# Two heads in one exponential: neighbouring PSUM banks read together in an attention stage

## The reference

```python
def _L0_attn_ref(hidden_states, cos, sin, wq, bq, wk, wv, bv, wo, bo):
    q = (hidden_states @ wq + bq).reshape(B, T, NH, HD).transpose(0, 2, 1, 3)
    k = (hidden_states @ wk).reshape(B, T, NH, HD).transpose(0, 2, 1, 3)
    v = (hidden_states @ wv + bv).reshape(B, T, NH, HD).transpose(0, 2, 1, 3)
    q, k = apply_rope(q, k, cos, sin)
    scale = 1.0 / jnp.sqrt(jnp.float32(HD))
    scores = jnp.einsum('bhqd,bhkd->bhqk', q, k) * scale
    attn = jax.nn.softmax(scores, axis=-1)
    out = jnp.einsum('bhqk,bhkd->bhqd', attn, v)
    out = out.transpose(0, 2, 1, 3).reshape(B, T, H)
    return out @ wo + bo

x = x + _L0_attn_ref(_layernorm(x), ...)
x = x + _L0_ffn_ref(_layernorm(x), ...)   # 16 experts, each takes its 128 best tokens of a batch; one shared expert
```

## Time and profile before

| | us |
|---|---|
| median of 3 runs | 2427.51 (2425.11 to 2431.14) |
| span of the profiled execution | 2427.3 |
| PE busy in the span | 2283.2 (94%) |
| DVE busy | 1891.8 (78%) |
| ACT busy | 1632.3 (67%) |
| POOL busy | 886.1 (37%) |

### The profile page before, as it was taken

One profiled execution on the slowest core, in us unless ns is written; L12 is line 12 of the kernel. 1 busy time (PEld: TensorE's weight loads), 2 busy tenths in 40 slices (PEclk: granted clock), 3 DMA queues, 4 the chain that ended last, 5 costly groups with the idle time before them and its releaser, 6 DMA issues. The chain is left out here.

```text
span 2427.3 us, 44076 instructions
## 1 busy us (share of the span) xinstructions
PE 2283.2 (94%) x16398; PEld 1340.3 (55%) x16398; DVE 1891.8 (78%) x3506; ACT 1632.3 (67%) x3168; POOL 886.1 (37%) x1223
## 2 busy tenths in 40 slices
PE   5899999999999999999999988899997999999996
PEld 4233334334334334334333323788886888888886
DVE  5999999999999999999999994466654555555553
ACT  2599999999999999999999987323323343333432
POOL 4051451451451451441542220000003666666664
PEclk8799999999999999999999999799998999999998
DMA  2000011010010010010010010332322545454443
GB/s 76 1 18 1 1 36 36 1 50 22 1 55 17 9 61 3 19 53 1 19 36 1 19 36 18 126 100 78 104 61 81 115 109 112 87 112 113 100 99 35
DMA packets 104364, 122.74 MB, mean 51 GB/s; under 512 B 7553, under 2 KB 91393, under 8 KB 104193
## 3 DMA queue, kind: packets, MB, share of 16 engines
q1 hardware_dynamic: 79616, 86.90, 11.2%
q0 software_dynamic: 24576, 33.57, 8.1%
HBM read 78.50 MB, written 41.94 MB: 50 GB/s over the span
## 5 line engine op out<-in xcount | busy, mean ns | idle before, releaser
L474 DVE TENSOR_REDUCE sb_MX<-ring 128x1 f32<-128x512 f32 x2048 | 1284.5, 681 | 82.0 <-PE ring L782 65.4
L606 ACT ACTIVATE sb_PR<-rot 128x512 f32<-128x512 f32 x2048 | 1123.3, 621 | 102.8 <-PE rot L793 92.3
L782 PE MATMUL ring<-sb_KT,sb_QT 32*128 32x512 bf16 x2048 | 517.1, 390 | 48.9 <-DVE sb_MX L474 36.5
L804 PE MATMUL pv<-sb_PR,sb_VA 128*32 128x512 f32 x4096 | 547.0, 606 | 2.9 <-ACT sb_OT L661 0.6
L782 PEld LDWEIGHTS ring<-sb_KT,sb_QT 32*128 32x128 bf16 x2048 | 128.1, 91 | 632.9 <-DVE sb_MX L474 565.8
L793 PE MATMUL rot<-sb_QT,sb_KT 32*128 32x512 bf16 x2048 | 422.1, 386 | 1.6
L1095 ACT ACTIVATE ex_GL<-ex_gu 128x512 f32<-128x512 f32 x128 | 76.4, 597 | 347.4 <-PE ex_gu L63 345.2
L1162 DVE TENSOR_TENSOR ex_HF<-ex_GL,ex_gu 128x512 f32<-128x512 f32 x128 | 87.5, 684 | 250.8 <-ACT ex_GL L1095 250.8
L1059 POOL DMA_INDIRECT out<-ex_YS,ex_rows_out x128 | 208.8, 1631 | 44.3 <-issue 43.8
L1016 POOL TENSOR_TENSOR ex_pool_scratch<-identity 128x1 f32<-128x1 f32 x96 | 35.1, 366 | 477.6 <-POOLq L859 332.0
L61 PE MATMUL ex_gu<-ex_XH,weights_high 128*128 128x512 f32 x512 | 200.4, 391 | 2.4 <-DVE ex_XL L1154 2.4
(11 more groups left out here) (168 smaller groups left out, 4272.2 us busy)
## 6 DMA issues: line engine op xcount, KB each, us to landing
sb_XA<-x SPq DMA_DIRECT2D x8, 1024.0 KB, 5.5
sb_XR<-x SPq DMA_DIRECT2D x8, 1024.0 KB, 5.8
out<-sb_XR SPq DMA_DIRECT2D x8, 1024.0 KB, 4.5
xn<-sb_XN SPq DMA_DIRECT2D x8, 1024.0 KB, 4.5
sh_XG<-xn SPq DMA_DIRECT2D x16, 512.0 KB, 5.5
sh_X<-out SPq DMA_DIRECT2D x16, 512.0 KB, 4.9
weights<-WgT SPq DMA_DIRECT2D x16, 512.0 KB, 4.0
weights<-WuT SPq DMA_DIRECT2D x16, 512.0 KB, 5.6
```

What stands on the lines that cost most here:

```text
L474: nc.vector.reduce_max(MX[:, unit % 2, half, j, qt % 4:qt % 4 + 1], ring[m % RING][:], AX.X).then_inc(ring_done, 1)
L606: out = nc.scalar.activation(PR[V % P_STEPS][:, j, :], R[:], ACT.Exp, scale=0.25)
L782: nc.tensor.matmul(ring[m % RING][:], QT[g][r, P * qt:P * qt + P], KT[g][r, 512 * half:512 * half + 512], start=True, stop=True, tile_posi ...
L804: out = nc.tensor.matmul(pv_bank[head(j), :], VA[b % 2][:, kt, 4 * g + j, :], PR[V % P_STEPS][:, j, :], start=(kt == 0), stop=(kt == TT - 1))
```

## The change

The four banks become one tensor of 128 x 4 x 512. Each step's four heads are cut into three pieces by the bank in which the step begins. Where that is bank 0, 1 or 2, heads 0 and 1 are one piece, in two neighbouring banks, and heads 2 and 3 one each; where it is bank 3, heads 0 and 1 are one each, and 2 and 3 are one piece. A piece of two heads is emptied by one exponential of 128 x 1024, which starts when both banks are full and frees both at its end. Items take banks in the same sequence as before. TensorE waits, for each bank, until its last user has been emptied, and tells ScalarE after the last head of a piece. The evacuation of `pv` stands behind the second piece.

```diff
+    PIECES = {}
+    for item in HEAD:
+        place(item)
+    for V in range(-LEAD, LAST):
+        if V >= 0:
+            at = (AT[-1][0] + AT[-1][1]) % ROT
+            PIECES[V] = ((0,), (1,), (2, 3)) if at == ROT - 1 else ((0, 1), (2,), (3,))
+            for heads in PIECES[V]:
+                place(("ex", V, heads[0]), len(heads))
+        for item in beside(V):
+            place(item)
...
+    EMPTIED, last_in = [], [0] * ROT
+    for n, (at, banks) in enumerate(AT):
+        EMPTIED.append(last_in[at:at + banks])
+        last_in[at:at + banks] = [n + 1] * banks
...
-        rot = [ctx.enter_context(nc.psum_tensor(f"rot{i}", [P, 512], F32)) for i in range(ROT)]
+        rot = ctx.enter_context(nc.psum_tensor("rot", [P, ROT, 512], F32))
...
-                    out = nc.scalar.activation(PR[V % P_STEPS][:, j, :], R[:], ACT.Exp, scale=0.25)
+                    out = nc.scalar.activation(PR[V % P_STEPS][:, j:j + banks, :], rot[:, at:at + banks, :], ACT.Exp, scale=0.25)
...
-                    for j in range(4):
-                        empty(("ex", V, j))
-                        if j == 2 and V >= 9 and V % 8 == 1:
+                    for n, heads in enumerate(PIECES[V]):
+                        empty(("ex", V, heads[0]))
+                        if n == 1 and V >= 9 and V % 8 == 1:
                             evacuate((V - 9) // 8)
...
-            def bank(item):
+            def bank(item, k=0):
                 n = PLACE[item]
-                if n >= ROT:
-                    pe.wait_ge(rot_done, n - ROT + 1)
-                return rot[n % ROT]
+                if EMPTIED[n][k]:
+                    pe.wait_ge(rot_done, EMPTIED[n][k])
+                return rot[:, AT[n][0] + k, :]
...
-                nc.tensor.matmul(R[:], KT[g][r, P * kt:P * kt + P], QT[g][r, 512 * qh:512 * qh + 512], start=True, stop=True,
-                                 tile_position=(r.start, 0)).then_inc(rot_full, 1)
+                out = nc.tensor.matmul(R, KT[g][r, P * kt:P * kt + P], QT[g][r, 512 * qh:512 * qh + 512], start=True, stop=True,
+                                       tile_position=(r.start, 0))
+                if j == heads[-1]:
+                    out.then_inc(rot_full, 1)
...
-                pe.wait_ge(rot_done, done(("ex", V, 3)))
+                pe.wait_ge(rot_done, done(("ex", V, PIECES[V][-1][0])))
```

More of the change, by code:

```diff
@@ L122, in attention, with place @@
             + [("lg", B - 1, half) for half in range(2)])
-    ORDER = HEAD + [item for V in range(-LEAD, LAST)
-                    for item in ([("ex", V, j) for j in range(4)] if V >= 0 else []) + beside(V)] + TAIL
+    ORDER, AT = [], []
+    def place(item, banks=1):
+        at = (AT[-1][0] + AT[-1][1]) % ROT if AT else 0
+        assert at + banks <= ROT
+        ORDER.append(item)
+        AT.append((at, banks))
+        return at
+    PIECES = {}
[9 more added lines that the diff above has]
+            place(item)
+    for item in TAIL:
+        place(item)
     PLACE = {item: n for n, item in enumerate(ORDER)}
     assert len(PLACE) == len(ORDER)
+    EMPTIED, last_in = [], [0] * ROT
+    for n, (at, banks) in enumerate(AT):
+        EMPTIED.append(last_in[at:at + banks])
+        last_in[at:at + banks] = [n + 1] * banks
     def done(item):
@@ L598, in empty @@
                 n = PLACE[item]
-                R = rot[n % ROT]
+                at, banks = AT[n]
+                R = rot[:, at, :]
                 kind = item[0]
@@ L614, in empty @@
                         act.wait_ge(as_ready, 4 * (b + 1))
-                    out = nc.scalar.copy(XT[:, h, 512 * half:512 * half + 512], R[:])
+                    out = nc.scalar.copy(XT[:, h, 512 * half:512 * half + 512], R)
                 elif kind == "q":
@@ L626, in empty @@
                     _, b, g, n = item
-                    out = nc.scalar.copy((QT, KT)[n][g][:], R[:].bitcast(BF16))
+                    out = nc.scalar.copy((QT, KT)[n][g][:], R.bitcast(BF16))
                 elif kind == "v":
@@ L635, in empty @@
                     qh = n % 2
-                    out = nc.scalar.copy(QT[n // 2][:, 512 * qh:512 * qh + 512], R[:].bitcast(BF16)[:, 0:512])
+                    out = nc.scalar.copy(QT[n // 2][:, 512 * qh:512 * qh + 512], R.bitcast(BF16)[:, 0:512])
                 elif kind == "ot":
@@ L640, in empty @@
                         act.wait_ge(ao_ready, unit)
-                    out = nc.scalar.copy(AR[:], R[:].rearrange("p (a c) -> p a c", c=QUAD)[:, :, 0:HD + 1])
+                    out = nc.scalar.copy(AR[:], R.rearrange("p (a c) -> p a c", c=QUAD)[:, :, 0:HD + 1])
                 elif kind == "bo":
@@ L738, in fill @@
                     for m in range(TT):
-                        out = nc.tensor.transpose(R[:].bitcast(BF16)[:, P * m:P * m + P],
+                        out = nc.tensor.transpose(R.bitcast(BF16)[:, P * m:P * m + P],
                                                   A[:, m, 4 * g:4 * g + 4, :].rearrange("p h c -> p (h c)"), identb[:])
@@ L790, in score_turned @@
                     pe.wait_ge(rot_done, done(("q2", b, unit % UNITS)))
-                R = bank(("ex", V, j))
+                heads = next(heads for heads in PIECES[V] if j in heads)
+                R = bank(("ex", V, heads[0]), heads.index(j))
                 r = head(j)
-                nc.tensor.matmul(R[:], KT[g][r, P * kt:P * kt + P], QT[g][r, 512 * qh:512 * qh + 512], start=True, stop=True,
-                                 tile_position=(r.start, 0)).then_inc(rot_full, 1)
+                out = nc.tensor.matmul(R, KT[g][r, P * kt:P * kt + P], QT[g][r, 512 * qh:512 * qh + 512], start=True, stop=True,
+                                       tile_position=(r.start, 0))
+                if j == heads[-1]:
+                    out.then_inc(rot_full, 1)
             def weigh_values(V):
```

## The result

The changed kernel takes 2464.4 us in the median of four runs (2463.2 to 2469.2) against 2427.1: ratio 1.0156, interval 1.0142 to 1.0171, slower by 37 us. The profile shown is of the slowest of the four runs; its span is 2467.5 us.

What follows compares the result with a forecast made beforehand. VectorE was taken to lead most of the time. Late fills cost 3 x 3.7 (batches 2, 4, 6) + 3 x 4.5 (1, 3, 5) + 4.5 (first and last) = 29 us; 2427.3 + 29 = 2456 us, range 2432 to 2475.

Steps and rivals of the forecast that it cites:

- The instruction: Each 1024-wide exponential on ScalarE lasts 1.02 us, against two single ones of 1.20 together.
- ScalarE's saving: One wide exponential replacing two saves 0.06 us of ScalarE's time, 31 us over 512 steps.
- Head 1 behind a pair (2,3): Next step's head 1 takes head 2's bank, freed late: fill 0.33 us late, at 8 to 14 places a batch.
- The extras' 0.8: Late extra fills in batches 1, 3 and 5 (steps 34, 40, 47, 55) add 0.8 us a batch.
- The extra behind a pair (0,1): The same step's extra fill takes head 0's bank: 0.42 us later where ScalarE is behind, no cost where TensorE leads.
- Slack and cover: Late fills cost only beyond their slack, and a fill 0.33 late vanishes where VectorE is behind.
- The 451.8 us: TensorE's waits for VectorE's maxima in 1200 us, 704 places; read as VectorE leading most of the time.
- The 116 waits ahead of L61: Places where TensorE waits for ScalarE to read a bank before an extra fill, 34.5 us in 1200 us.
- The third rival: Lateness uses up the covers in a 2.47 us loop: 2495 us in full, 2475 halfway; chance 0.13.
- ScalarE's saving as a gain: Rival: ScalarE is the bound, so its saving makes the kernel faster, 2396 us, or 2417; chance 0.06.
- That all is covered: Rival: TensorE's waits for VectorE swallow all late fills, 2427 us within 7; chance 0.11.
- Lateness feeding on itself: The third rival: pair end, extra fill, heads and pair form a 2.47 us loop, 0.42 shorter before; chance 0.13.

Runs made afterwards that it cites:

- the run without a fall: The changed kernel with single exponentials instead of pairs in steps 46 to 49 of each batch, around the gate logits: 2458.9 us.

## Why the prediction was right

**Size and sign.** 2456 was forecast, 2464.4 came, and the range held it. The sum has 3.7 us for batches 2, 4 and 6 (measured 3.7), 4.5 for 1, 3 and 5 (4.8) and 4.5 for the first and last (3.1 and, without a stretch at the lower clock, 2.0 to 2.6). That makes 29 forecast and about 31 measured.

**The term that was missing** is TensorE's clock, which I took at 1.00 throughout: 3.9 us in batch 1 and some 7.1 in batch 7 (9.7 against the 2.6 of the run without a fall) in the profiled execution, some 5.5 in the median (2464.4 against 2458.9 without pairs at the gate logits).

**The instruction.** 1.02 was taken for a pair; the mean is 1.04. ScalarE's saving was near what the rows gave: L606's busy time of 1123.3 fell to 1086.4 on the page, by 37 us where 31 was taken, and ScalarE still stands idle more, as its waits for scores grew from 75.2 to 110.5 us.

**Head 1 behind a pair (2,3):** right to the hundredth where it was worked out (0.33 late, rows of 919.28). Its sum over batches 1, 3 and 5 was too large: alone it is 2.6 there, not 3.7. The extras' 0.8 was too small: they make up the other 2.2 of the 4.8. That 4.5 still came out near 4.8 is luck, two errors that cancel.

**The extra behind a pair (0,1):** right in the step that was worked out (1.12 instead of 0.70).

**Slack and cover.** Right: 235 pairs with slack cost nothing, and with VectorE's lead taken away a full batch loses 5.9 to 6.4 us instead of 3.7 to 4.8. The reading behind it was wrong. The 451.8 us that put VectorE in the lead are mostly the weight loader's idle time under the pv matmuls, so VectorE is ahead by much less than I thought. The 116 waits ahead of L61 are of the same sort: 89 are of 0.23 us, which the loader shows at 897.18 too, where it waits for nothing that the profile shows. The third rival priced all 116 as late places; the sum used neither number.

**Rivals.** ScalarE's saving as a gain is refuted by the 235 pairs and by the halved reduces; it is real only as a part given back of a loss, some 1 us a batch. That all is covered is refuted by the time. Lateness feeding on itself would have shown in batches that lose more towards their end or in each other's wake. Batches 2, 4 and 6 lose the same 3.7, and within batch 4 the steps fall back in jumps of at most 0.43 us, 0.34 at step 6 and 0.42 at step 60, with some of it made up in between.

No version with pairs beat the kernel before: where they are free, they gain nothing.

## What to carry to other kernels

An instruction that empties two buffers frees the first only when it has emptied both. So ask for each buffer how long after its reader's end the next writer starts: fused reading is free where that slack exceeds the added duration (here 0.42 + 0.05 us), and what exceeds the slack goes through the writer's queue to whoever waits behind it. A saving on an engine that is 92% busy was worth nothing here, as its partners wait for its buffers, not for its throughput. Before a wait of the weight loader is read as TensorE waiting, look whether matmuls run under it. And an added wait of 0.15 us went with falls of the clock, so look at the granted clock of every batch, not at its mean.

## What the runs showed of the hardware

TensorE's clock fell to its lower level in a stage in which TensorE is nearly always busy: 134.74 of the 141.20 us ahead of the fall in batch 1, and all of the row of 10.3 us at 0.50. Right ahead of the fall stand an idle time of 0.15 us and sixteen matmuls of 16 columns (1.96 us). With the idle time, 8 of 28 such places had a fall; the same matmuls without it had none in 56 places, among them all of the kernel before. A 1024-wide exponential over two banks takes 1.04 us in the mean where one of 512 takes 0.61, 0.43 more. Copies of 512 and 256 columns (602 and 409 ns in the kernel before) differ by 0.19, which would make 0.39 for 512 columns: by this estimate, reading across the bank boundary costs some 0.05 us at most.
